# Expert routing rewritten: raw rows gathered and normalised before use, one-hots in bf16, picks in two parts

## The reference

```
x = x + gnn(layernorm(x))                         # attention over the neighbours
# layer 0 (H = 512)                               # layer 1 (H = 1024)
p = softmax(xn @ gate_w)                          p = softmax(xn @ Wr)
top2_vals, top2_idx = top_k(p, 2)                 weights = top_p / top_p.sum()
out = sum over the two of val * expert(xn)        xe = layernorm(xn) * ln_g[e] + ln_b[e]
expert(v) = gelu(v @ W1 + b1) @ W2 + b2           out = sum over the two of weight * expert(xe)
x = x + out
```

## Time and profile before

| | us |
|---|---|
| median of 3 runs | 1790.25 (1790.2 to 1791.03) |
| the profiled execution | 1787.74 |
| its span, first to last instruction | 1786.0 |
| PE busy in the span | 1660.1 (93%) |
| DVE busy | 931.6 (52%) |
| ACT busy | 955.8 (54%) |
| POOL busy | 351.8 (20%) |

### The profile page before, as it was taken

One profiled execution on the slowest core, in us unless ns is written; L12 is line 12 of the kernel. 1 busy time (PEld: TensorE's weight loads), 2 busy tenths in 40 slices (PEclk: granted clock), 3 DMA queues, 4 the chain that ended last, 5 costly groups with the idle time before them and its releaser, 6 DMA issues.

```text
span 1786.0 us, 41369 instructions
## 1 busy us (share of the span) xinstructions
PE 1660.1 (93%) x13364; PEld 1535.9 (86%) x13365; DVE 931.6 (52%) x2186; ACT 955.8 (54%) x2194; POOL 351.8 (20%) x314
## 2 busy tenths in 40 slices
PE   4799999999799999589999999999988999999998
PEld 3588888878789999479999999999978999999997
DVE  4578868778612222568888878877780111111111
ACT  1143444435334433368989989899743444444443
POOL 2110000000156666320000000000002333333332
PEclk9899999999899999799999999999999999999999
DMA  9990000003478887400000000000375666666664
GB/s 160 108 176 10 10 10 9 28 28 125 143 190 208 229 209 186 159 10 18 14 14 19 9 19 18 10 19 14 110 281 175 176 177 179 182 186 186 176 176 97
DMA packets 86495, 189.98 MB, mean 106 GB/s; under 512 B 13737, under 2 KB 60585, under 8 KB 77577
## 3 DMA queue, kind: packets, MB, share of 16 engines
q1 hardware_dynamic: 53705, 139.39, 23.5%
q0 software_dynamic: 31360, 48.45, 17.2%
q10 hardware_dynamic: 1344, 1.05, 0.2%
HBM read 188.98 MB, written 33.11 MB: 124 GB/s over the span
## 4 chain that ended last, share of the span: by engine, by line
PE 52%; DVE 3%; ACT 1%; issue 1%; DMA 1%; DVEq 0%; POOL 0%; ACTq 0%; POOLq 0%
PE bank L1774 24%; PE bank L2285 12%; PE bank L2324 11%; PE bank L707 1%; PE bank L710 1%; PE bank L2292 1%; ACT arena L1476 1%; DVE arena L1612 0%; PE bank L2173 0%; PE bank L697 0%; DVE arena L1610 0%; DMA arena<-xe 0%; DVE X L2107 0%; PE bank L2180 0%; PE bank L2165 0%
## 5 line engine op out<-in xcount | busy, mean ns | idle before, releaser
L1774 PE MATMUL bank<-arena 128*128 128x195 bf16 x5408 | 467.1, 248 | 14.2 <-DVE arena L1612 10.9
L1774 PEld LDWEIGHTS bank<-arena 128*128 128x128 fp8e4 x5408 | 463.8, 97 | 17.6 <-issue 16.7
L1476 ACT ACTIVATE arena<-arena,m_row 128x512 fp8e5<-128x512 f32 (+1 forms) x672 | 401.5, 678 | 44.5 <-DVE arena L1612 32.8
L2285 PEld LDWEIGHTS bank<-X,arena 128*128 128x128 f32 x2832 | 337.1, 194 | 8.7 <-issue 2.3
L2388 DVE TENSOR_TENSOR arena<-bank,X 128x256 f32<-128x256 f32 x118 | 50.1, 425 | 563.7 <-PE bank L2324 563.7
L2285 PE MATMUL bank<-X,arena 128*128 128x128 f32 x2832 | 339.2, 277 | 0.1
L2324 PE MATMUL bank<-arena,X 128*128 x1416 | 325.2, 379 | 2.5 <-ACT X L2362 2.0
L1319 PE MATMUL bank<-arena 128*128 (+1 forms) x1352 | 312.1, 386 | 15.1 <-DVE arena L1225 15.1
L1319 PEld LDWEIGHTS bank<-arena 128*128 128x128 f32 x1352 | 252.5, 191 | 55.7 <-issue 20.9
L2324 PEld LDWEIGHTS bank<-arena,X 128*128 128x128 f32 x1416 | 259.9, 190 | 33.7 <-issue 3.1
L2362 ACT ACTIVATE X<-bank,arena 128x128 f32<-128x128 f32 x708 | 196.0, 379 | 70.2 <-issue 61.5
(11 more groups left out here) (249 smaller groups left out, 1346.2 us busy)
## 6 DMA issues: line engine op xcount, KB each, us to landing
arena<-m1w SPq DMA_DIRECT2D x67, 1024.0 KB, 10.6
arena<-m0w SPq DMA_DIRECT2D x67, 512.0 KB, 7.1
xs<-X SPq DMA_DIRECT2D x4, 1664.0 KB, 7.1
arena<-qd SPq DMA_DIRECT2D x25, 256.0 KB, 3.1
arena<-adjT POOLq DMA_DIRECT2D x13, 448.0 KB, 12.9
arena<-adjT POOLq DMA_DIRECT2D x13, 384.0 KB, 10.8
xe<-zeros POOLq DMA_DIRECT2D x1, 3456.0 KB, 21.7
X<-x_in SPq DMA_DIRECT2D x2, 1664.0 KB, 11.5
```

The lines of the kernel that those rows point to most:

```text
L1476: last = a.activation(self.sign[slot].bitcast(F8W)[:, q * W:q * W + nt * P], self.row[r][:, 0:nt * P], ACT.Sigmoid, scale=STEEP, bias=self ...
L1774: last = pe.matmul(bank[rb * NT + n][:, kind * KW:(kind + 1) * KW], self.split[slot][kind].bitcast(F8)[:, q * W + n * P:q * W + (n + 1) * ...
L2285: last = pe.matmul(bank[2 * s + c // 4][:, c % 4 * P:(c % 4 + 1) * P], self.W1[s][:, k * HID + c * P:k * HID + (c + 1) * P], self.rxt[s][: ...
```

## The change

- X is no longer scaled in place. xs gets the raw rows, and rows of xs become 260 numbers long (ROW): the last four hold the row's scale, its shift, the weight of its first expert and the difference of the second's from it. SP stores the raw rows pair by pair in layer 0 (`gelu_sync`) and in three parts in layer 1, as soon as they are final; W2's eight parts go out in one run. The four columns (`row_cols`) are stored by one transfer when the weights are known (`cols_stored`).
- The picks are made in two parts: tiles 0 to 19 as soon as their logits are there, then tiles 20 to 25, whose logits go to a bank of their own (PICK_PARTS).
- One-hots are in bf16, with the 13 token columns innermost. Instead of row number and weight, two small integers are recovered by the products: a code (tile of the token, plus 32 for a second choice) and the token's place in its tile. ScalarE makes its half of `hot_tile` in one operation per round. VectorE works `slot_row` out of code and place in six operations; `slot_w` first holds only whether the choice is the second one.
- The tile table is made after the fourth round.
- After a gather VectorE works out the tile's weights from the gathered columns and normalises the tile in `rx` (`norm`, semaphore `rx_ready`, for which TensorE now waits). Tiles 0 to 3 are normalised ahead of the loop, tile g + 4 after the two operations on tile g's result.
- Unread products: 20 instead of 48 after the logits, 80 instead of 96 after the counts, 6 after each of the first three one-hot rounds and 36 after the fourth.
- POOL makes three index tables (767, 1664 and 52 numbers) instead of one of 128.

```diff
-            def gelu_sync(self, sp):
+            def gelu_sync(self, sp, rows_stored):
...
+                    sp.dma_start(xs[at(i * 2 * P, 2 * P), 0:D].rearrange("(t p) d -> p t d", p=P),
+                                 X[:, at(i * 2 * D, 2 * D)].rearrange("p (t d) -> p t d", d=D)
+                                 ).then_inc(rows_stored, 16)
...
-                load_w2(range(4))
-
-                for g in range(2):
-                    sp.wait_ge(self.x_scaled, (g + 1) * PAIRS)
-                    sp.dma_start(xs[g * PAIRS * P:(g + 1) * PAIRS * P, :].rearrange("(t p) d -> p t d", p=P),
...
-                load_w2(range(4, 8))
+                n = w2m.shape[1] // 8
+                for g in range(8):
+                    sp.dma_start(self.W2[:, g * n:(g + 1) * n], w2m[:, g * n:(g + 1) * n]).then_inc(self.w2_loaded, 16)
+                sp.wait_ge(self.weights_ready, 1)
+                sp.dma_start(xs[0:NP, D:ROW].rearrange("(t p) c -> p t c", p=P), self.row_cols
+                             ).then_inc(self.cols_stored, 16)
...
-                with v.Fori(0, PAIRS) as i:
-                    for s in range(2):
...
-                        v.tensor_scalar(xv, xv, self.scale_x[:, at(t, 1)], self.shift_x[:, at(t, 1)],
-                                        ALU.mult, ALU.add).then_inc(self.x_scaled, 1)
...
+                for (a, b), logits_bank in zip(PICK_PARTS, (bank[2], bank[7])):
+                    pick_part(a, b, logits_bank)
...
-                    v.tensor_tensor(self.hot_place[b].rearrange("p (q m) -> p q m", m=P),
-                                    self.place_no.rearrange("p (o m) -> p o m", o=1).to_broadcast([P, PAIRS, P]),
-                                    over(self.place_of[:, q], P), ALU.is_equal)
+                    v.tensor_tensor(self.hot_place[b].rearrange("p (m q) -> p m q", q=PAIRS),
+                                    self.place_all.rearrange("p (m q) -> p m q", q=PAIRS),
+                                    row(self.place_of[:, q], P), ALU.is_equal)
...
-                    for q in range(PAIRS):
-                        n = c * PAIRS + q
-                        last = a.activation(self.hot_tile[b][:, (2 * q + 1) * G:(2 * q + 2) * G],
-                                            self.equal[b][:, q * G:(q + 1) * G], ACT.Identity,
-                                            scale=self.weight_of[:, n:n + 1])
+                    a.wait_ge(self.hot_used[b], c // 2 + 1)
+                    last = a.activation(self.hot_tile[b][:, PAIRS * G:2 * PAIRS * G], self.equal[b], ACT.Identity,
+                                        scale=row_id[:, 0:1])
...
+                    place = self.hot_place[c % 2].rearrange("p (m q) -> p m q", q=PAIRS)
+                    tile = self.hot_tile[c % 2].rearrange("p (g q) -> p g q", q=PAIRS)
                     for q in range(PAIRS):
-                        last = pe.matmul(bank[5][:, 0:2 * SLOT_TILES],
-                                         self.hot_place[c % 2][:, q * P:(q + 1) * P],
-                                         self.hot_tile[c % 2][:, q * 2 * SLOT_TILES:(q + 1) * 2 * SLOT_TILES],
+                        last = pe.matmul(bank[5][:, 0:2 * SLOT_TILES], place[:, :, q], tile[:, :, q],
                                          start=False, stop=False, skip_group_check=True)
                     last.then_inc(self.hot_used[c % 2], 1)
+                    idle_products(6 if c < 3 else 36)
...
-                pool.wait_ge(self.slots_ready, 2)
-                for s in range(2):
-                    pool.wait_ge(self.xn_stored[s], 16)
+                pool.wait_ge(self.slots_ready, 1)
+                pool.wait_ge(self.rows_stored, self.n_stored)
+                pool.wait_ge(self.cols_stored, 16)
...
+                def norm(g, s, nth):
+
+                    x = self.rx[s]
+                    v.wait_ge(self.rx_loaded[s], 16 * nth)
+                    v.scalar_tensor_tensor(out=slot_w[:, at(g, 1)], in0=slot_w[:, at(g, 1)], scalar=x[:, D + 3:D + 4],
+                                           in1=x[:, D + 2:D + 3], op0=ALU.mult, op1=ALU.add)
+                    v.tensor_scalar(x[:, 0:D], x[:, 0:D], x[:, D:D + 1], x[:, D + 1:D + 2], ALU.mult, ALU.add
+                                    ).then_inc(self.rx_ready, 1)
...
+                    if not isinstance(g, int) or g + 4 < RUN_TILES:
+                        norm(g + 4, q, j + 2)
```

More of the change, by code:

```diff
@@ L1865, in __init__ @@
                 k += 4 * T
[L1866 to L1870, removed]
+                self.tile_of = words(k, T).bitcast(BF16)
                 k += T
+                self.place_of = words(k, T).bitcast(BF16)
+                k += T
+                self.slots = words(k, SLOT_TILES)
+                k += SLOT_TILES
                 self.scale_x = words(k, T)
@@ L1925, in __init__ @@
                 self.places_ready = sem(tag + "places_ready")
-                self.xn_stored = [sem(f"{tag}xn_stored{s}") for s in range(2)]
+                self.rows_stored = sem(tag + "rows_stored")
+                self.n_stored = (3 if second_norm else PAIRS) * 16
+                self.cols_stored = sem(tag + "cols_stored")
                 self.ysum_ready = sem(tag + "ysum_ready")
@@ L1983, in step @@
                     v.wait_ge(r, n[0])
-                scale = rstd[:, :]
+                scale, shift = self.row_cols[:, :, 0], self.row_cols[:, :, 1]
                 if self.second_norm:
@@ L2011, in route_vector @@
+                v.scalar_tensor_tensor(out=shift, in0=mv[:, 0:T], scalar=-1.0, in1=scale, op0=ALU.mult, op1=ALU.mult)
                 TE = T * E
-                lg3 = self.logits.rearrange("p (t e) -> p t e", e=E)
                 w3 = self.work.rearrange("p (t e) -> p t e", e=E)
[L2014 to L2018, removed]
@@ L2054, in route_vector @@
                 step(v.tensor_tensor(p3, i3.rearrange("p e t -> p t e"), w3, ALU.subtract))
-                step(v.tensor_tensor(p3, p3, spread_t(self.base), ALU.add))
+                step(v.tensor_tensor(p3, p3, spread_t(self.base, T), ALU.add))
                 step(v.tensor_tensor(self.posx, bank[3][:, 0:TE], self.posx, ALU.add))
@@ L2116, in route_vector @@
                     v.wait_ge(self.hot_used[k], 3)
-                step(v.tensor_scalar(self.spare, bank[5][:, 0:G], 0.0, spare_row[:, :],
-                                     ALU.is_equal, ALU.mult))
-                v.scalar_tensor_tensor(out=slot_row[:, :], in0=bank[5][:, 0:G], scalar=1.0,
-                                       in1=self.spare, op0=ALU.subtract, op1=ALU.add).then_inc(self.slots_ready, 1)
-                v.tensor_copy(slot_w[:, :], bank[5][:, G:2 * G]).then_inc(self.slots_ready, 1)
+                slots = self.slots
@@ new lines, in route_vector @@
+                codes, places = bank[5][:, 0:G], bank[5][:, G:2 * G]
+                v.tensor_scalar(slots, codes, float(P), None, ALU.mult)
+                step(v.tensor_scalar(slot_w[:, :], codes, float(SECOND_CODE), None, ALU.is_ge))
+                step(v.tensor_tensor(slots, places, slots, ALU.add))
+                step(v.tensor_scalar(self.spare, slots, 0.0, spare_row[:, :], ALU.is_equal, ALU.mult))
+                step(v.scalar_tensor_tensor(out=self.spare, in0=slot_w[:, :], scalar=-float(SECOND), in1=self.spare,
+                                            op0=ALU.mult, op1=ALU.add))
@@ L2124, in route_scalar @@
+                v.scalar_tensor_tensor(out=slot_row[:, :], in0=slots, scalar=1.0, in1=self.spare,
+                                       op0=ALU.subtract, op1=ALU.add).then_inc(self.slots_ready, 1)
             def route_scalar(self, a, last_gelu=None):
```

202 lines of the change are left out of this document (107 added, 95 removed).

## The result

| | before | after |
|---|---|---|
| median, us | 1790.22 (8 runs) | 1807.16 (8 runs, 1797.96 to 1810.01) |
| ratio to before, 95% interval | | 1.0091 (1.0074 to 1.0108) |
| the profiled execution, us | 1787.74 | 1808.58 |
| its span, us | 1786.0 | 1806.8 |

The change makes the kernel slower by 0.9%, 16 us, where 24 us less was forecast. I cut both traces at the same events; the last column is the term of the forecast. Last row, last logit, last pick and slots are ends of rows, first one-hot and results are starts; a result is VectorE's addition of the bias (line 2388, in the changed kernel 2414).

The account below looks back on a forecast made before the run. TensorE bounds the expert stages, VectorE's routing chain delays the first gathers. Sum: -2.1 - 10.8 - 4.9 - 9.6 + 1.0 + 2.0 = -24.4 us, from 1790.25 to 1766 us; 8-in-10 range 1757 to 1798.

Parts of the forecast that it names:

- The step that failed: Routing in both layers: POOL's two longer index fills run while VectorE picks, cost zero.
- One-hots: First one-hot to slots: 1.87 us a VectorE round, 11.5 us in all; -10.8 us in layer 0, -9.6 in layer 1.
- A: Rival: one-hots at one element per cycle, a round stays 3.5 us, +6.6 per layer, 1779 us; chance 0.12.
- D: Rival: one-hots read 26 bytes apart cost TensorE double per pass, 3.8 us a round, 17.9 to slots, 1779; chance 0.10.
- both then lie beside VectorE's round: One-hot rounds: TensorE's thirteen passes and ScalarE's one activation fit beside VectorE's 1.87 us, if strided operands cost no more.
- the ring: Tile loop: result, scatter, gather, normalising close over two tiles, 7.05 us against TensorE's 7.54 in layer 0; +2 us taken.
- rival C: Layer 0's ring sets the pace: half of the way to +36 us gives 1783, the whole 1800; chance 0.12.
- The column store: Before the first gather: one transfer of 3328 16-byte pieces, 8.3 us of cover; zero taken, other end 19 us per layer.
- B: Rival: the 16-byte column store comes 19 us late per layer, 1804 us; chance 0.24.
- Picks: Routing, picks in two parts: -2.1 us in layer 0, -4.9 in layer 1.
- the line: Picks: price per operation from 0.40 us at 208 columns and 0.21 at 59; 0.34 taken for 160 columns, 0.22 for 48.
- W1's zero: First tile: W1 asked for only 1.5 us ahead of the slots costs 0 to +3.5 us; 0 taken.

Follow-up runs that it names:

- Fills alone: Kernel before, with POOL also filling three larger tables (767, 1664 and 52 numbers, bf16) at the same place, into unread memory: 1811.77 us, ratio 1.0131.
- late fills: Changed kernel, with POOL filling its three index tables only after VectorE has written the scales of the rows: 1786.96 us, ratio 0.9960.
- bare rounds: On the late fills, without the six unread products that follow each of the first three one-hot rounds: 1780.76 us, ratio 0.9955.
- the table sooner: Changed kernel with late fills, gathers one tile sooner, bare rounds, and the tile table made after the second round again: 1771.08 us, ratio 0.9896.
- the order of before: Changed kernel, all tables and one-hots with token column outermost again, bf16, so TensorE reads both operands at step one: 1790.05 us, ratio 0.9979.
- the stream packed: Same edits as the table sooner, plus the two tile one-hots made token column outermost, streamed numbers side by side: 1767.10 us, ratio 0.9876.

## Why the prediction was wrong

- **The step that failed** is the sentence that POOL's longer index fills run while VectorE picks, at zero. They start with the last row, when VectorE makes the statistics that ScalarE's root, its copies and so TensorE wait for. Fills alone: +23.5 us; fills moved: -23.5. The forecast had neither the collision nor the clock that falls behind a stall of 1.5 to 3 us, and none of its rivals was this. The Trainium skill ("SBUF — State Buffer", Who interferes with whom) has the rule: copies, casts and operations on one tensor and constants can take the port pair that VectorE shares with GpSimd, whoever is first holds it for the whole instruction, and an operation on two tensors meets only a GpSimd reader. The rows agree with it: 3.17 and 4.81 us against 0.20, and 1.49 for the copy.
- **One-hots**: A's price was refuted, VectorE ran at 0.59 and 1.09 us. D was right, and I had given it 0.10: a round is 4.1 us (D: 3.8), the slots come 18.8 and 19.0 us after the first one-hot (D: 17.9). The mis-sized term is the cover "both then lie beside VectorE's round": TensorE's thirteen products take 3.02 us, not less than 1.87. It is not the clock: the thirteen took 3.02 us in layer 0's first round, at a granted 1.00, and 3.02 in the second, at 0.50.
- **Layer 0's loop**: the ring was the right mechanism, as rival C; its size was 9.1 us, not 2, and the reason that I gave against it (later gathers meet less traffic) did not hold it off. Moving the issue by one tile removed it.
- **The column store**: zero was right, B fell. It lands in 5.6 us, against a cover that D made longer.
- **Picks** were right: with the late fills the last pick comes 4.29 and 4.30 us after the last logit, 2.2 and 5.1 less than before (forecast 2.1 and 4.9). One price in it does not follow: the line gives 0.20 us for 48 columns, not 0.22; the operations were 0.24 apart, so the sum came out.
- **The first tile**: normalising and the wake-up cost 0.9 us from slots to TensorE's turn in layer 0 (3.78 to 4.70; forecast 0.5), and up to the first result 0.4. W1's zero held while the rounds were long. With bare rounds layer 1's first gather, issued 2.9 us behind the loads, took 6.3 us; with the table sooner, 8.4 us behind them, 3.0. The forecast's upper end of 3.5 us does not follow from its 10.6 and 5, which leave 5.6.
- **The range** ended at 1798: it took in slow stores and a slow loop, but no effect ahead of the picks.

## What to carry to other kernels

Of every instruction that is moved or made longer, ask what runs on the engines beside it at its new time, not only what its own engine does; a helper that is off the path can hold up the short operations that are on it. Here a TensorE that stood for 1.5 to 3 us ran the next 20 us at half its clock, so price a stall with what follows it. A layout is chosen for the writer and both readers at once: here the order that nearly doubled VectorE's rate more than doubled the products' price, and the sum hardly moved (18.8 us from the first one-hot to the slots, 18.1 in the order of before).

## What the runs showed of the hardware

- VectorE's TENSOR_SCALAR and COPY of one tensor wait for a POOL fill that is running (3.17, 4.81, 1.49 us instead of 0.2); an operation on two tensors does not (0.19). Not every form with one tensor waits: eight BATCH_NORM_STATS2 took 2.71 us beside the first fill, 0.34 each, as before it (1.40 for four).
- A fill's price goes by its pattern: 1664 bf16 numbers take 4.33 us in runs of 13 equal numbers and 1.58 us in rising runs of 128; 767 take 1.99 us in runs of 13 and 1.04 in rising runs of 59. Whether the length of the run or the equal numbers cost was not tested apart.
- VectorE writes bf16 numbers across at 4.5 to 4.7 ns each (7.55 us for 1664, 3.58 for 767), ScalarE at 4.9 (3.74 for 767 instead of 0.93).
- Thirteen products whose streamed operand steps 26 bytes take 3.02 us at either level of the clock; with the stream packed they take 1.00 us at 1.00 and 1.50 at 0.50. The same step in the weights costs next to nothing: with both packed it is 0.86 and 1.46 us.
- During the strided products the granted clock fell although TensorE was busy: 10.00 of 10 us at 0.58 (late fills, 460 to 470 us), where the kernel before had 7.66 of 10 at 1.00. It fell in the packed rounds too (with the token column outermost 0.50 in 470 to 480 us, 8.21 of 10 busy), so the step is not shown to be the cause; what brings it down there was not tested.
